# A gated cross-attention and expert block on one core: V kept on chip, K and Q rows copied chip to chip, maxima rows sent between them, one transpose moved

## The reference, cut to what matters

```python
x = x + tanh(g_xattn) * xattn(layernorm(x), ctx)      # x: 4 x 512 x 256, ctx the same, fp32
x = x + tanh(g_ffn)   * ffn(layernorm(x))

# xattn: 16 heads of 16 columns
q = (x @ W_q);  k, v = split(ctx @ W_kv)
attn = softmax(einsum('bhqd,bhkd->bhqk', q, k) * 16 ** -0.5)
out = einsum('bhqk,bhkd->bhqd', attn, v) @ W_proj + b_proj

# ffn: router picks the best 2 of 8 experts per token, each silu(x Wg) * (x Wu) @ Wd; a shared expert is added
out = shared(xf) + sum_e comb[:, e] * expert_e(xf)
```

## Time and profile before

| | |
|---|---|
| median of three runs | 518.9 us (518.71 to 519.51) |
| profiled execution | 517.66 us, span 515.9 us |
| PE busy | 491.2 us (95% of the span) |
| DVE busy | 304.8 us (59%) |
| ACT busy | 264.0 us (51%) |
| POOL busy | 174.0 us (34%) |
| mean granted PE clock | 0.989 of full speed |

### The profile page before, as it was taken

One profiled execution on the slowest core, in us unless ns is written; L12 is line 12 of the kernel. 1 busy time (PEld: TensorE's weight loads), 2 busy tenths in 40 slices (PEclk: granted clock), 3 DMA queues, 4 the chain that ended last, 5 costly groups with the idle time before them and its releaser, 6 DMA issues.

```text
span 515.9 us, 8196 instructions
## 1 busy us (share of the span) xinstructions
PE 491.2 (95%) x2876; PEld 305.6 (59%) x2876; DVE 304.8 (59%) x549; ACT 264.0 (51%) x418; POOL 174.0 (34%) x193
## 2 busy tenths in 40 slices
PE   8999899999999999999969999999999999999992
PEld 7655433233223333234445367599999999999991
DVE  3766779889899898994564796223333333333321
ACT  2666277777677777776524203114444444444430
POOL 4500177772221111111000003005656655556642
PEclk9999999999999999999989999999999999999997
DMA  7999519987864666300022002122344434443432
GB/s 253 309 280 257 216 43 232 300 193 202 218 172 99 174 174 174 83 1 23 0 81 83 2 0 83 41 83 51 63 62 68 66 63 66 67 64 62 61 43 31
DMA packets 44882, 58.60 MB, mean 114 GB/s; under 512 B 6352, under 2 KB 36688, under 8 KB 44336
## 3 DMA queue, kind: packets, MB, share of 16 engines
q1 hardware_dynamic: 29536, 36.12, 25.8%
q0 software_dynamic: 7488, 10.23, 12.9%
q10 hardware_dynamic: 7824, 11.81, 7.0%
HBM read 37.89 MB, written 20.05 MB: 112 GB/s over the span
## 4 chain that ended last, share of the span: by engine, by line
PE 67%; DMA 18%; DVE 6%; issue 3%; ACT 2%; SPq 1%; POOLq 1%; POOL 0%; DVEq 0%
PE ps L1097 52%; DMA out<-unit_region 17%; PE ps L1183 11%; DVE neg_max L809 3%; PE ps L1103 1%; ACT ctx_region L668 1%; DVE rows L866 1%; DMA unit_region<-qk_parts 1%; PE ps L1427 1%; SPq L341 1%; PE ps L1312 1%; DVE up_region L793 0%; SPq L360 0%; POOLq L83 0%; PE ps L1175 0%
## 5 line engine op out<-in xcount | busy, mean ns | idle before, releaser
L809 DVE TENSOR_REDUCE neg_max<-ps 128x2 f32<-128x1024 f32 x128 | 151.5, 1212 | 27.1 <-PE ps L1097 26.7
L668 ACT ACTIVATE ctx_region<-ps 128x512 f32<-128x512 f32 x256 | 139.7, 595 | 54.1 <-PE ps L1097 53.9
L1097 PE MATMUL ps<-unit_region 96*128 96x512 bf16 (+1 forms) x512 | 132.2, 381 | 5.8 <-ACT ctx_region L668 1.9
L1097 PEld LDWEIGHTS ps<-unit_region 96*128 96x128 bf16 (+1 forms) x512 | 46.7, 97 | 115.8 <-ACT ctx_region L668 73.8
L1097 PE MATMUL ps<-unit_region,ctx_region 128*128 128x128 f32 (+1 forms) x968 | 113.8, 274 | 0.0
L1097 PEld LDWEIGHTS ps<-unit_region,ctx_region 128*128 128x128 f32 (+1 forms) x968 | 110.5, 189 | 0.6 <-issue 0.3
L559 POOL DMA_INDIRECT out<-unit_region x39 | 61.8, 1585 | 55.6 <-DMA out<-unit_region 50.8
L1097 PE MATMUL ps<-dn_region,unit_region 128*128 (+1 forms) x330 | 78.2, 379 | 0.0
L532 POOL DMA_INDIRECT unit_region<-x_rows,unit_region x39 | 38.6, 989 | 116.8 <-DVE unit_region L1051 79.7
L726 ACT COPY ctx_region<-up_region 128x1536 f32 x39 | 57.3, 1472 | 34.8 <-PE ps L1097 31.9
L1072 DVE TENSOR_TENSOR unit_region<-unit_region,ps 128x384 f32<-128x384 f32 x39 | 21.6, 554 | 83.5 <-ACT unit_region L743 66.3
(11 more groups left out here) (146 smaller groups left out, 375.1 us busy)
## 6 DMA issues: line engine op xcount, KB each, us to landing
up_region<-in_w_upT ACTq DMA_DIRECT2D x9, 768.0 KB, 4.5
qk_parts<-up_region SPq DMA_DIRECT2D x32, 192.0 KB, 3.4
unit_region<-qk_parts SPq DMA_DIRECT2D x32, 192.0 KB, 4.2
v_rows<-dn_region SPq DMA_DIRECT2D x4, 1024.0 KB, 6.0
unit_region<-qk_parts SPq DMA_DIRECT2D x32, 128.0 KB, 4.4
unit_region<-v_rows SPq DMA_DIRECT2D x16, 256.0 KB, 5.3
dn_region<-in_w_downT ACTq DMA_DIRECT2D x9, 384.0 KB, 5.6
ctx_region<-in_ctxT SPq DMA_DIRECT2D x4, 512.0 KB, 10.6
```

Of the source, the lines that this page charges most:

```text
L668: nc.scalar.activation(probs[:, k % 8, :], bank(4 + k % 2), ACT.Exp).then_inc(exp_done, 1)
L809: nc.vector.tensor_reduce(neg_max[:, s, 2 * p:2 * p + 2], bank(2 * (p % 2), 2), AX.X, ALU.max, negate=True).then_inc(max_done, 1)
L1097: return nc.tensor.matmul(o_, w, m, start=start, stop=stop)
```

## The change

1. V stays in SBUF. Each batch has a home of its own (`v_home`: three in `dn_region`, one where `v_unit` was), PE reads it there, and `v_rows` and its DMAs are gone. PE waits for `v_done` in place of `v_in`. POOL sets the columns of ones in four pieces in place of one.
2. `qk_parts` is gone. Every block of 16 rows is copied from `parts` to `k_unit` or `q_unit` by a DMA of its own, 64 KB each, SBUF to SBUF: six for K and six for Q of a unit (`LOADS` is 12, it was 6).
3. SP's order inside a slot: K rows of unit u + 4, maxima rows of unit u + 2, Q rows of unit u + 4. Before, the maxima rows stood behind all rows of the unit. The wait for `pv_done` in front of the K rows is the same.
4. `turn_back` stands behind the seventh maximum of a slot, not behind the third.
5. ACT's 18 loads of experts' weights are spread by `UP_AT` and `DOWN_AT` over slots 1 to 15 (they stood in nine of slots 1 to 11), with waits for `unit_in` and `pv_done` that guard the memory they overwrite.
6. PE's loop over slots 1 to 12 is written out, and the wait for the last whole K and Q (`whole_sb`) moves from ahead of slot 0 to its `turn_max`.

```diff
-K_RUNS = ((0, 1, 2), (0,), (0, 1))
-Q_RUNS = ((0, 1), (0, 1, 2), (0,))
+K_PARTS = (0, 1, 2, 0, 0, 1)
+Q_PARTS = (0, 1, 0, 1, 2, 0)
...
+PARTS_READ = {2: 0, 5: 1, 9: 2, 13: 3}
+UP_AT = (2, 3, 5, 6, 9, 10, 13, 14, 7)
+DOWN_AT = (13, 14, 15, 5, 6, 9, 10, 11, 1)
...
-LOADS = len(K_RUNS) + len(Q_RUNS)
+LOADS = len(K_PARTS) + len(Q_PARTS)
...
+        V_AT = (2 * DC * T, 2 * DC * T + v_words, 0)
+
+        def v_home(b):
+            home = (dn_region[:, V_AT[b]:V_AT[b] + v_words] if b < len(V_AT) else unit_region[:, 4 * HG * T:unit_words])
+            return home.rearrange("p (k h w) -> p k h w", k=TB, h=H)
...
-            def load_rows(b, g, a, dst, runs):
-                row = 0
-                for run in runs:
-                    n = len(run)
-                    src = qk_parts[a, bass.ds(b, 1), g, 0:n, :, :].rearrange("a j (d h) n -> (a j d) (h n)", h=HG)
-                    to = dst[row:row + n * HD, g, :, :].rearrange("p h n -> p (h n)")
-                    sp.dma_start(to, src).then_inc(unit_in[g], 16)
-                    row += n * HD
...
+            def load_rows(b, g, a, dst, order):
+                half = P // 2 * (g % 2)
+                for i, j in enumerate(order):
+                    sp.dma_start(dst[i * HD:(i + 1) * HD, g, :, :], parts[half:half + P // 2, b, a, j, g // 2, :]
+                                 ).then_inc(unit_in[g], 16)
...
-            for b in range(1, B):
-                for g in range(NG):
-                    u = (b - 1) * NG + g
-                    send_max(u + 1, (g + 1) % NG)
-                    if 1 <= u <= len(SPLIT_ORDER):
-                        a, late = SPLIT_ORDER[u - 1]
-                        send_parts(a, late, k_out[late] if a else q_out[late])
-                    if g == 0:
-                        sp.wait_ge(k_out[b], 16 * QK_OUTS)
-                        sp.wait_ge(q_out[b], 16 * QK_OUTS)
-                        sp.wait_ge(v_out[b], 16)
-                    sp.wait_ge(pv_done, u * TB + TB)
-                    load_unit(b, g)
-            for u in range(UNITS - 3, UNITS):
+            sp.wait_ge(low_done, QK_ORDER.index((1, 0)) + 1)
+            for g in range(2):
+                load_rows(0, g, 1, k_unit, K_PARTS)
+            sp.wait_ge(low_done, QK_ORDER.index((0, 0)) + 1)
+            for g in range(2):
+                load_rows(0, g, 0, q_unit, Q_PARTS)
+            for g in range(2, NG):
+                load_rows(0, g, 1, k_unit, K_PARTS)
+                load_rows(0, g, 0, q_unit, Q_PARTS)
+            send_max(0, 0)
+            send_max(1, 1)
+            for u in range(UNITS - NG):
+                b, g = u // NG + 1, u % NG
+                if b == 1:
+                    sp.wait_ge(low_done, len(QK_ORDER) // 2)
+                elif g == 0:
+                    for a in range(2):
+                        sp.wait_ge(split_done, SPLIT_ORDER.index((a, b)) + 1)
+                sp.wait_ge(pv_done, u * TB + TB)
+                load_rows(b, g, 1, k_unit, K_PARTS)
+                send_max(u + 2, (u + 2) % NG)
+                load_rows(b, g, 0, q_unit, Q_PARTS)
+            for u in range(UNITS - 2, UNITS):
                 send_max(u, u % NG)
...
-                for r in range(1, NG + 1):
-                    if r < NG:
-                        load_expert(b * 3 + r - 1)
-                    exp_slot(b * NG + r, r % NG)
-            for u in range(UNITS - 3, UNITS):
+            for u in range(1, UNITS):
+                if u in PARTS_READ:
+                    for g in range(NG):
+                        act.wait_ge(unit_in[g], 16 * LOADS * (PARTS_READ[u] + 1))
+                if u in UP_AT:
+                    load_up(UP_AT.index(u))
+                if u in DOWN_AT:
+                    if u > NG:
+                        act.wait_ge(pv_done, (u - 1) // NG * NG * TB)
+                    load_down(DOWN_AT.index(u))
                 exp_slot(u, u % NG, more_max=u + 1 < UNITS)
...
-                    if p == 2 and u % 2 == 0:
+                    if p == 6 and u % 2 == 0:
                         turn_back(u - 1)
...
-                pe.wait_ge(v_in[s], 16 * (bu + r // NG + 1))
+                pe.wait_ge(v_done, u // NG + 1)
...
                         if first:
                             pe.wait_ge(nmT_sb, 1)
+                            pe.wait_ge(whole_sb, len(WHOLE_ORDER))
...
-            pe.wait_ge(whole_sb, len(WHOLE_ORDER))
             slot(0, 0, 0, first=True)
-            with pe.Fori(0, B - 1) as b:
-                for r in range(1, NG + 1):
-                    slot(b * NG + r, b, r)
+            for u in range(1, UNITS - 3):
+                slot(u, (u - 1) // NG, (u - 1) % NG + 1)
```

More of the change, by code:

```diff
@@ L105, in build @@
         resid = dn_region[:, 0:2 * DC * T].rearrange("p (a c n) -> p a c n", a=2, c=DC)
-        v_sb = dn_region[:, 2 * DC * T:2 * DC * T + 2 * TB * H * VW].rearrange(
-            "p (s k h w) -> p s k h w", s=2, k=TB, h=H)
-        unit_words = 2 * 4 * HG * T // 2 + 4 * TB * HG * VW
+        v_words = TB * H * VW
+        unit_words = 4 * HG * T + v_words
         unit_region = sb("unit_region", [P, unit_words])
@@ L271, in build @@
         split_step, split_done = sem("split_step"), sem("split_done")
-        k_out = [sem(f"k_out{b}") for b in range(B)]
-        v_out = [sem(f"v_out{b}") for b in range(B)]
-        q_out = [sem(f"q_out{b}") for b in range(B)]
         unit_in = [sem(f"unit_in{s}") for s in range(4)]
-        v_in = [sem(f"v_in{s}") for s in range(4)]
         pair_ps = sem("pair_ps")
@@ L464, in _ @@
             pool.wait_ge(rows_done, 1)
-            nc.gpsimd.memset(v_sb[:, :, :, :, HD:VW], 1.0).then_inc(v_ones, 1)
-            pool.wait_ge(v_ones, 1)
+            for n, b in enumerate((0, 1, 3)):
+                nc.gpsimd.memset(v_home(b)[:, :, :, HD:VW], 1.0).then_inc(v_ones, 1)
+                pool.wait_ge(v_ones, n + 1)
             nc.gpsimd.iota(lag[:, :], pattern=[[16, BLOCK_PAIRS], [0, 2]], base=0, channel_multiplier=0,
@@ L513, in split_whole @@
                                         ).then_inc(split_done, 1)
+            pool.wait_ge(low_done, len(QK_ORDER) // 2)
+            nc.gpsimd.memset(v_home(2)[:, :, :, HD:VW], 1.0).then_inc(v_ones, 1)
+            pool.wait_ge(v_ones, B)
             split_max(0)
@@ L610, in copy_v @@
                     act.wait_ge(v_ones, 1)
-                if b >= 2:
-                    act.wait_ge(v_out[b - 2], 16)
-                nc.scalar.copy(v_sb[:, b % 2, :, :, 0:HD],
+                if b == 2:
+                    act.wait_ge(low_done, len(QK_ORDER) // 2)
+                nc.scalar.copy(v_home(b)[:, :, :, 0:HD],
                                bank(V_BANK, 2).rearrange("p a (k h w) -> p (a k) h w", k=2, h=H)).then_inc(v_done, 1)
@@ L647, in _, with load_up, load_down @@
             whole_q(3)
[L649 to L654, removed]
+            def load_up(e):
+                act.dma_start(w_up[:, e, :, :], w_upT[e, :, :].rearrange("(c p) f -> p c f", p=P)).then_inc(w_ffn_in, 16)
+            def load_down(e):
+                act.dma_start(w_dn[:, e, :, :], w_downT[e, :, :].rearrange("(c p) n -> p c n", p=P)).then_inc(w_ffn_in, 16)
             def copy_max(u):
@@ L1182, in pv @@
                 for h in range(HG):
-                    last = nc.tensor.matmul(bank(6)[h * VW:(h + 1) * VW, :], v_unit[:, s, kt, h * VW:(h + 1) * VW],
+                    last = nc.tensor.matmul(bank(6)[h * VW:(h + 1) * VW, :], v_home(u // NG)[:, kt, u % NG * HG + h, :],
                                             probs[:, (kt * HG + h) % 8, :], start=kt == 0, stop=kt == TB - 1,
@@ L1273, in _ @@
             pe.wait_ge(ones_rows, 1)
+            pe.wait_ge(v_ones, B)
             pe.wait_ge(rowsT_sb, B)
[L1275 removed]
             slot(0, 0, 0, first=True)
[L1277 to L1279 removed]
+            for u in range(1, UNITS - 3):
+                slot(u, (u - 1) // NG, (u - 1) % NG + 1)
             def project(t):
```

22 lines of the change are left out of this document (removed).

## The result

The change made the kernel slower by far more than forecast: 580.5 us median (four runs, 575.28 to 583.92) against 519.2 (four runs, 518.71 to 519.89), ratio 1.115, 95% interval 1.110 to 1.121. The profiled execution is one of 580.96 us, span 579.2.

The account below looks back on a forecast made before the run. PE's own work was taken as the bound. Start -1.7 and Q rows behind the maxima rows +13.9 gave +12.2: 529.9 us for the profiled execution, 531 as median; 8-in-10 range 517.5 to 549.

Parts of the forecast that it names:

- The bound: Attention slots 1 to 12: PE's own work bounds the kernel, busy 140.6 of 143 us; no transfer does.
- the start: Start of attention: 1.10 us won at the first pair's wait, 0.6 from the moved `whole_sb` wait, together 1.7.
- The deciding term: Q rows behind maxima rows in SP's queue: period 13.04 us, some 1.3 stall in each of slots 2 to 13, +13.9.
- T: The moment `pv_done` frees a home in a slot, 1.67 us behind the slot's start.
- The issue i: SP's time to issue one Q copy behind the maxima rows, taken as 0.50 us, between ends of 0.316 and 0.62.
- The landing L: Time for the sixth Q copy to land in a slot, taken as 2.2 us, between ends of 1.6 and 4.3.
- the landing of 4.3: Rival for the Q copies in the slots: they land late, period 15.14 us, time 556; chance 0.08.
- the weights' loads at 0: ACT's loads of experts' weights: they move by a slot or so, the last some 20 us before the shared expert; 0.
- The clock: Rival: PE's clock falls in the slots' stalls; if every slot paid 1.5 us, the time is 549; chance 0.12.
- the likeliest case: The forecast itself: stalls of some 1.3 us in slots 2 to 13, median 531 us; chance 0.60.
- `turn_back` cost nothing: Moved transpose in the slots: 0 where DVE catches up during a stall of 1.3 us; +2.2 without that cover.

## Why the prediction was wrong

The bound and the start were read rightly: the first pair's wait went, and with the `whole_sb` wait the first slots came 2.3 us earlier, where I had 1.7. The deciding term was also the right one, with its formula: the period of a quiet slot at full clock is 8.34 + 5i + L, the chain to T + 4.88 did not move there, and the twelve stalls are where they were said to be. The forecast of slower held; the size was off by five times (12.2 against 61.3), and the time lies far above 549, where the range ended. Three terms were wrong.

The issue i: 0.50 was taken, halfway between loads out of device memory and the maxima rows. It is 0.594, and 0.63 with the gap to the next. Of the two ends, the row that also goes from SBUF to SBUF (0.589) was right, and there was no ground to average it with one that shares only the target. That is 5 x 0.13 x 12 = 8 us.

The landing L, the step that failed most. "In that part of a slot nothing else is in the queue" was true of SP's queue only. In quiet slots L is 2.6, not 2.2 (5 us over twelve). But ACT issues 384 KB, 768 KB or both of weights towards the end of a slot, and in the kernel before those fell where no copy was wanted soon. In slot 5, whose T is 124.08, they were issued here:

```profile
133.45 0.37 ACTq L650 DMA_DIRECT2D up_region<-in_w_upT  x1
```

That is T + 9.4, when the rows issued by T + 3.3 had had 6 us to land. Under the changed order the Q copies are issued from T + 6.7 to T + 10.5 and land until T + 12.5, so the weights fly beside them. Three Q copies took 5.7 us there, and the six stalls with weights are 17.2 us longer than quiet ones. The rows for it could have been had: this one, and the landing of 4.3 that I set aside as a rival with 0.08. I had costed the weights' loads at 0 by when they are needed, and not by whom they delay. The experiment with the weights later prices this at 26 us, clock included.

The clock: the rival was held at 0.12 because the stall of the likeliest case was 1.3 us. With the true i and L, and the weights, the stalls are 2.0 to 6.7. The earlier trace rows had a fall behind 2.42 us and none behind 1.27; between the two I had nothing, and the clock fell behind 1.98 and 2.10. The profile has 21.8 us for it, more than the 18 of the rival in which every slot paid 1.5: a slot at the low clock was 1.5 to 3.1 us longer than one of 11.72. The three were not independent: each made the next likelier, and I added them as separate cases. The first two terms, these 17.2 and the clock come to some 52 us, against the 51 that lie between the forecast of 12.2 and the 63.3 of the traces.

The rule of the Trainium skill (DMA: Bandwidth & Descriptors, Issuing engines are not separate DMA queues) that the time to issue is usually small beside the DMA itself did not carry over to a row of small copies: one issue took 0.594 us and its landing 2.6, but six issues took 3.78, more than a landing. The same section states that DMAs from all engines run on the same 16 engines and interleave; the Q copies at 5.7 us beside the weights agree with it, and it was the sentence to weigh.

`turn_back` cost nothing, as forecast; but the reason given, that a stall would cover it, was not needed, since alone, without such stalls, it costs nothing that its run can tell either.

## What to carry to other kernels

Before a transfer is put behind another in a queue, work out two moments: when the last piece lands and when the first reader asks for it. Here the wait stood 2 us ahead of the first use, and moving it was worth 36 us. Many small copies cost the queue their number times the issue, whatever they save in memory traffic; they belong where the queue has time, as for the first batch. And what another engine's queue sends in the same stretch counts in full.

## What the runs showed that I had not expected

A 64 KB copy from SBUF to SBUF takes SP 0.594 us to issue, more than the loads of 64 to 192 KB from device memory (median 0.421), and lands in 2.6 us where those took 4.3, though beside more traffic (DMA share 0.70, here 0.28). POOL issues a maxima row in 0.49 us, no slower than SP's 0.59, but the row then takes 2.4 us to land, where SP's in the changed kernel took 1.7. And PE's clock fell after some stalls of about 2 us and not after others that were longer (in the changed kernel behind 1.98 and not behind 2.32; with the weights later behind 2.32, at 1.63 us, and not behind 2.87). What decides it no run here shows.
